# First stage of an RWKV + MoE kernel: the transposed FFN input is scaled from the transposed LayerNorm output, and the routing moves into its own round

## The reference

```python
xn = layernorm(x)                                  # no gain, eps 1e-5
prev = concat([xn[:, 1:2], xn[:, :-1]], axis=1)    # the token before
k, v, r, g = [(xn + (prev - xn) * tm_i) @ W_i.T for i in "kvrg"]
ek, ekv, gate = exp(k), exp(k) * v, sigmoid(r) * sigmoid(g)   # kept for the output stage
z = w_norm * xn * rsqrt(mean(xn**2) + 1e-6)        # input of the FFN, all 4096 tokens
probs = softmax(z @ w_router); top 4 of 32 experts  # each expert takes at most 256 tokens, in order
shared gate = sigmoid(z @ w_shared_gate)
```

## Time and profile before

| what | value |
|---|---|
| median of 3 runs | 1773.22 us (1773.07 to 1777.1) |
| the profiled execution, its own time | 1772.68 us |
| its span, first to last instruction | 1770.9 us |
| PE busy | 1690.1 us, 95% of the span |
| DVE, POOL, ACT busy | 1217.8, 878.3, 660.5 us |
| share of the chain that ended last | PE 79%, DVE 10%, waits for nothing shown 5% |

### The profile page before, as it was taken

The page is one execution under the profiler, slowest core; times in us unless marked ns, Lnnn a source line. Parts: engine busy times, 40 slices in busy tenths (PEclk is TensorE's granted clock), DMA queues, the critical chain, the costliest instruction groups (busy, mean ns, idle before and its releaser), DMA issues.

```text
span 1770.9 us, 26936 instructions
## 1 busy us (share of the span) xinstructions
PE 1690.1 (95%) x8752; PEld 1444.6 (82%) x8752; DVE 1217.8 (69%) x1798; ACT 660.5 (37%) x1086; POOL 878.3 (50%) x730
## 2 busy tenths in 40 slices
PE   4699999999889999999998899999999999999998
PEld 4578877788779999999997688888788888888887
DVE  4777778776635555555556978687686768778776
ACT  3344454454446566656653322112121212112121
POOL 2477887777635444544435635243252525344251
PEclk7799999999989999999999999999999999999999
DMA  6224434233366666666677656554554343343431
GB/s 225 95 72 159 152 131 154 103 136 119 127 228 245 248 229 222 245 248 229 222 260 238 208 186 208 169 170 155 172 167 164 125 140 122 122 157 108 149 109 46
DMA packets 130379, 299.36 MB, mean 169 GB/s; under 512 B 23724, under 2 KB 35116, under 8 KB 129776
## 3 DMA queue, kind: packets, MB, share of 16 engines
q1 hardware_dynamic: 110832, 264.58, 41.8%
q0 software_dynamic: 19456, 33.67, 6.7%
HBM read 233.57 MB, written 81.36 MB: 178 GB/s over the span
## 4 chain that ended last, share of the span: by engine, by line
PE 79%; DVE 10%; issue 5%; DMA 2%; POOL 1%; ACT 1%; DVEq 0%; SPq 0%; POOLq 0%; ACTq 0%
PE bank L1738 24%; PE bank L1116 15%; PE bank L1752 12%; PE bank L789 10%; PE bank L1143 8%; PE bank L1769 5%; PE bank L739 2%; PE bank L1108 2%; DVE mixf L553 2%; PE bank L757 1%; DVE st L518 1%; POOL slot_tokens L341 1%; DVE s_wg L1642 1%; DVE sr L572 1%; DVE s_ek L1586 0%
## 5 line engine op out<-in xcount | busy, mean ns | idle before, releaser
L789 PE MATMUL bank<-mix,w 128*128 128x512 f32 x1536 | 375.9, 402 | 25.9 <-POOL mix L333 12.8
L789 PEld LDWEIGHTS bank<-mix,w 128*128 128x128 f32 x1536 | 291.8, 193 | 93.2 <-issue 20.2
L1738 PE MATMUL bank<-s_zT,s_wg 128*128 128x512 f32 x1056 | 258.8, 395 | 9.8 <-DVE s_wg L1642 9.4
L1738 PE MATMUL bank<-s_zT,s_wu 128*128 128x512 f32 x1056 | 256.2, 392 | 2.8 <-DVE s_act_g L1547 1.9
L1752 PE MATMUL bank<-s_wd,s_h 128*128 128x512 f32 x1056 | 254.0, 389 | 0.8 <-DVE s_h L1553 0.8
L1738 PEld LDWEIGHTS bank<-s_zT,s_wg 128*128 128x128 f32 x1056 | 200.4, 190 | 54.6 <-DVE s_wg L1642 12.2
L1738 PEld LDWEIGHTS bank<-s_zT,s_wu 128*128 128x128 f32 x1056 | 199.4, 189 | 45.9 <-issue 2.3
L1752 PEld LDWEIGHTS bank<-s_wd,s_h 128*128 128x128 f32 x1056 | 198.3, 188 | 42.8 <-issue 1.2
L942 POOL TENSOR_TENSOR e_wg<-e_g_in,e_wg 128x1408 fp32r<-128x1408 f32 x32 | 103.5, 3233 | 219.4 <-ACT e_wg L967 219.4
L333 POOL TENSOR_TENSOR mix<-mixf,mix 128x512 fp32r<-128x512 f32 x120 | 156.6, 1334 | 68.6 <-ACT mix L413 68.1
L1373 POOL DMA_INDIRECT s_picked<-y_rows,s_slot x128 | 141.5, 1106 | 84.4 <-DVE s_total L1603 44.7
(11 more groups left out here) (149 smaller groups left out, 2388.4 us busy)
## 6 DMA issues: line engine op xcount, KB each, us to landing
s_wu<-wu_split SPq DMA_DIRECT2D x77, 512.0 KB, 3.4
e_g_in<-in_w_gate SPq DMA_DIRECT2D x32, 704.0 KB, 4.4
e_u_in<-in_w_up SPq DMA_DIRECT2D x32, 704.0 KB, 5.9
zT_tiles<-zT SPq DMA_DIRECT2D x32, 512.0 KB, 2.6
e_d_in<-in_w_down SPq DMA_DIRECT2D x32, 512.0 KB, 6.7
y_rows<-e_y SPq DMA_DIRECT2D x32, 512.0 KB, 2.9
s_zT<-zT_tiles SPq DMA_DIRECT2D x32, 512.0 KB, 5.9
x_in<-in_x SPq DMA_DIRECT2D x32, 256.0 KB, 4.2
```

Source lines behind the costliest of these rows:

```text
L789: last = pe.matmul(pj[m][:], w[i][:, w_part, k, m * P:(m + 1) * P], mix[:, i % 2, k, x_part, :], start=(k == 0 and q == 0), stop=(k == KC ...
L1738: last = pe.matmul(into[:], w[:, w_part, k, :], zT[:, :, x_part, k, :], start=(q == 0 and k == 0), stop=(q == 2 and k == KC - 1))
```

## The change

1. z is no longer transposed. xn is (now four tiles in SBUF, two PSUM banks in turn); r2 is turned once a round with four transposes of a broadcast column (`turn_r2`), and `make_zf` on DVE multiplies xnT, the norm weight as a per-partition scalar and the turned r2. High and low parts of all 512 tokens follow; they are stored as two parts of 1 MB.
2. The scores hold the router weights still (68 columns) and move 512 tokens: 8 matmuls a round. ACT copies the result to SBUF (`keep_score`), PE turns it back with four transposes (`turn_score`).
3. Scores, `choose`, `count` and `assign` of sequence b all run in round b. Scatters: 7 between the `mix_lo` calls of G and of the next K, 4 behind those, 5 in the next round. The last round has all 16 of its own, after 5 of round 6.
4. x is loaded two rounds ahead; r2 and the scales have two halves.
5. All small constants come in one array of 516 columns, loaded from ACT's queue; weights are loaded ahead of x of sequence 1. POOL makes the low parts of the R and G weights, behind `mix_lo` of V.
6. Expert 1's weights are loaded when R of the last round is done; the low part of expert 0's gate weight moves from POOL to DVE.

The core of the diff:

```diff
-        def z_lo(b, j):   # from tz, the transposed z in PSUM, by tile
+        def make_zf(b, half, k):
...
+            wait(dve, zl_made, n - 1)
+            dve.scalar_tensor_tensor(zf[:, k % 2, :], xnT[half][:, k, 1:T + 1], norm_col[:, k:k + 1], rb[:],
+                                     ALU.mult, ALU.mult).then_inc(zf_made, 1)
+        def make_zT(b, half):
+            make_zf(b, half, 0)
+            make_zf(b, half, 1)
+            z_lo(b, 0)
+            make_zf(b, half, 2)
+            z_lo(b, 1)
+            make_zf(b, half, 3)
+            z_lo(b, 2)
+            z_lo(b, 3)
...
# tensor
+        def turn_r2(b, half):
+            pe.wait_ge(pow_step, (b + 1) * POWS)
+            wait(pe, zf_made, b * KC)
+            for j in range(NT):
+                last = pe.transpose(rb[:, j * P:(j + 1) * P], r2[:, half, j:j + 1].to_broadcast([P, P]), ident)
+        def score(b):
+            pe.wait_ge(zl_made, (b + 1) * KC)
             for x_part in (1, 0):
                 for k in range(KC):
-                    last = pe.matmul(rp_lg[:, j * 2 * RW:(j + 1) * 2 * RW], zT[:, j % 2, x_part, k, :],
-                                     wr[:, k].rearrange("p q e -> p (q e)"),
+                    last = pe.matmul(sb, wr[:, k].rearrange("p q e -> p (q e)"), zT[x_part][:, k, :],
...
+        def one_round(b, half):
             project(b, K_, 0)
+            score(b)
             project(b, K_, 1)
+            turn_score(b)
             project(b, V_, 0)
+            turn_xn(b + 1, 0)
+            turn_xn(b + 1, 1)
             project(b, V_, 1)
+            count(b)
+            turn_xn(b + 1, 2)
+            turn_xn(b + 1, 3)
+            turn_r2(b + 1, 1 - half)
             project(b, R_, 0)
             project(b, R_, 1)
             project(b, G_, 0)
             project(b, G_, 1)
...
# gpsimd
+        def one_round(b, half):
+            mix_lo(b, V_)
+            norm_scales(b + 1, 1 - half)
+            mix_lo(b, R_)
+            scatter(b - 1, MORE, NT * TOPK)
+            mix_lo(b, G_)
+            scatter(b, 0, SOME)
+            mix_lo(b + 1, K_)
+            scatter(b, SOME, MORE)
+        def last_round():
+            mix_lo(LAST, V_)
+            scatter(LAST - 1, MORE, NT * TOPK)
+            mix_lo(LAST, R_)
+            scatter(LAST, 0, NT * TOPK)
+        SOME, MORE = 7, 11
...
# vector, one_round
+            make_gate(b - 1, 2)
+            make_gate(b - 1, 3)
             for k in range(KC):
                 make_mix(b, half, V_, k)
+            norm_stats(b + 1)
+            for k in range(KC):
+                make_mix(b, half, R_, k)
+            choose(b)
+            make_z(b + 1, 1 - half, 0)
+            make_z(b + 1, 1 - half, 1)
             make_ekv(b, 0)
             make_ekv(b, 1)
+            make_z(b + 1, 1 - half, 2)
+            make_z(b + 1, 1 - half, 3)
+            keep_scales(b + 1, 1 - half)
+            make_mix(b, half, G_, 0)
+            make_mix(b, half, G_, 1)
             make_ekv(b, 2)
             make_ekv(b, 3)
             make_mix(b, half, G_, 2)
             make_mix(b, half, G_, 3)
+            assign(b)
+            for k in range(KC):
+                shift_difference(b + 1, 1 - half, k)
+            for k in range(KC):
+                make_mix(b + 1, 1 - half, K_, k)
+            make_zT(b + 1, 1 - half)
             make_gate(b, 0)
             make_gate(b, 1)
...
# vector, last_round: V mixes, R mixes, choose, assign, ekv 0 and 1, G mixes, ekv 2 and 3, mix_lo of G, first_weights
...
# sync, expert stage
+        def second_weights():
+            sp.wait_ge(shared["r_done"], B * KC)
+            load(1, 1)
...
-            sp.wait_ge(gathered[0], 32)
-            sp.wait_ge(shared["g_done"], B * KC)
-            load(1, 1)
```

More of the change, by code:

```diff
@@ L350, in gpsimd @@
         pool.wait_ge(setup_pool, 4)
[L351 to L378, removed]
@@ L474, in one_round @@
                 mix_hi(b, R_, k)
[L475 to L487 removed]
+            make_xn(b + 1, 1 - half, 2)
@@ L661, in vector, with first_round @@
+        weight_lo(K_)
+        for j in range(3):
+            keep_turned(0, 0, j)
         for k in range(KC):
             shift_difference(0, 0, k)
[L663 removed]
             make_mix(0, 0, K_, k)
[L665 to L673 removed]
+        def first_round():
+            for k in range(KC):
+                make_mix(0, 0, V_, k)
+            weight_lo(V_)
+            make_zT(0, 0)
+            norm_stats(1)
+            keep_scales(0, 0)
+            dve.wait_ge(n_loaded, 16)
+            make_z(0, 0, 0)
+            make_z(0, 0, 1)
+            make_ekv(0, 0)
+            make_ekv(0, 1)
+            for k in range(KC):
+                make_mix(0, 0, R_, k)
+            make_z(0, 0, 2)
+            make_z(0, 0, 3)
+            make_ekv(0, 2)
+            make_ekv(0, 3)
+            choose(0)
+            for k in range(KC):
+                make_mix(0, 0, G_, k)
+            assign(0)
+            for k in range(KC):
+                shift_difference(1, 1, k)
+            make_mix(1, 1, K_, 0)
+            make_mix(1, 1, K_, 1)
+            make_gate(0, 0)
+            make_gate(0, 1)
+            make_mix(1, 1, K_, 2)
+            make_mix(1, 1, K_, 3)
+            make_zT(1, 1)
+            keep_scales(1, 1)
+            for j in range(NT):
+                make_z(1, 1, j)
@@ L687, in one_round @@
-            if not more:
-                for k in range(KC):
-                    mix_lo(b, R_, k)
+            norm_stats(b + 1)
+            for k in range(KC):
+                make_mix(b, half, R_, k)
+            choose(b)
+            make_z(b + 1, 1 - half, 0)
+            make_z(b + 1, 1 - half, 1)
             make_ekv(b, 0)
             make_ekv(b, 1)
-            if more:
-                z_lo(b + 1, 0)
-            if not before:
-                weight_lo(G_)
-                assign(b)
+            make_z(b + 1, 1 - half, 2)
@@ L708, in one_round @@
             make_mix(b, half, G_, 3)
-            if not more:
-                for k in range(KC):
-                    mix_lo(b, G_, k)
-                first_weights()
-            if more:
-                z_lo(b + 1, 2)
-                z_lo(b + 1, 3)
-                for k in range(KC):
-                    shift_difference(b + 1, 1 - half, k)
-                make_mix(b + 1, 1 - half, K_, 0)
-                make_mix(b + 1, 1 - half, K_, 1)
-                choose(b + 1)
+            assign(b)
```

646 lines of the change are left out of this document (372 added, 274 removed).

## The result

1764.13 us, median of 4 runs (1763.06 to 1766.36), against 1773.83 us (1773.07 to 1777.1) for the kernel before on the same chip: 0.9946 times, 95% interval 0.9931 to 0.9961. The change is faster, by 9.7 us where 56 were forecast, and the time lies outside the range of 1699 to 1740. The profiled execution took 1764.3 us, 1.8 outside its span.

A forecast was written before the change was run, and what follows sets the result against it. PE was taken to bound the rounds, with POOL and DVE not far below. 1772.7 - 37.7 (start) - 19.4 (middle rounds) + 8.2 (last round) - 7.4 (hand-over) = 1716.4, as a median 1717 us; range 1699 to 1740.

The forecast's parts named there:

- part 1: Middle rounds: 50.5 us each, between 48.8 and 54.1; six rounds 305 us against 324.4, a gain of 19.4 us.
- the 47.7 us of the DVE chain: Middle round: DVE's work from K0's start to the gate for the next K0, ending 1.1 us before PE needs it.
- I had added 3.5: Middle round, DVE up to the G mixes: 3.5 us for waits on POOL's SBUF turn and the store of z.
- rival 1: Middle rounds: DVE is the bound, `z_lo` and G mixes wait for whole POOL fours; 53 us a round, 1732; chance 0.18.
- Rival 2: Middle rounds: a new wait, K0's gate behind `make_zT`, eats the gain; period 54.1 us, 1738; chance 0.07.
- the 2 us of the prediction: Late in round 1: 2 us for a first score that finds zT late, DVE coming from a long round 0.
- Part 2: Start and round 0: K0 of round 0 at 20 us, of round 1 at 77 instead of 114.7; gain 37.7 us.
- Part 3: Last round: the slot table comes later, K0 to the end of the first turn takes 60 us; loss 8.2 us.
- Part 4: Hand-over to the experts: idle before expert 0's first down projection goes and it gets shorter; gain 7.4 us.
- rival 3: Round 0 stays long: K0 of round 1 at 88 us, 1728 in all; chance 0.10.
- rival 4: Slower than before: a 5.26 us gap with each scatter batch makes POOL's cycle 64.3 us, 1800; chance 0.04.

The follow-up runs named there:

- s9: The changed kernel with nine scatters instead of seven on POOL ahead of the four `mix_lo` of the next K; 1741.36 us.
- s9_ends: s9 with the last round's R low parts on DVE and, in round 0, four scatters ahead of round 1's K low parts; 1738.75 us.
- gates_s4_ends: Changed kernel with gates ahead of `make_zT`, four scatters before K's run, last R low parts on DVE, four round 0 scatters ahead of next K's `mix_lo`; 1757.56 us.
- g_weight_later: The changed kernel with POOL's low part of the G weight moved behind the low parts of R's input in round 0; 1763.45 us.
- late_w1: The changed kernel with expert 1's weights loaded after the gather of expert 0 and the end of G, as before the change; 1771.79 us.

## Why the prediction was wrong

**The step that failed** is in part 1, the order on DVE: "The last two `z_lo` of DVE lie in it. If they get in between two calls it costs 1.5 us, if they wait for all of them 4 us". With the 47.7 us of the DVE chain these are rounds of 49.2 and 51.7 us, and the 50.5 I took lies between them. Both were too short. In the round from K0 at 207.38 the stall is 5.1 us beyond the `z_lo`'s own length, a `z_lo` waits 0.45 us for its high part, and `make_zT` begins at 43.6 instead of 41.4: 47.7 + 2.2 + 0.4 + 5.1 = 55.4 us, the measured round. By my own times (`make_zT` from 41.4 on, POOL's run from 43.8 to 48.9) the second `z_lo` already lay in the run, and it is the one that is hit. The 2.2 us were lost although I had added 3.5: the turned scores come 1.6 us late, since K0 is slow, and runs of `mix_lo` hold `choose` (8.5 us for 5.3) and two mixes of G (2.85 us for 1.4). POOL's run begins at 47.0, 3.2 us late, for it waits for the slots; its seven scatters took the forecast time (9.2 us, 245.26 to 254.43, for 9.1). PE's work was right: from K0 to the end of G1 it is 50.3 us, of which the slow K0 makes 1.6 (7.2 us to the first score, 5.6 in s9), so 48.7 for my 48.8. That a late gate can also slow the clock was not priced.

The argument against rival 1 drew a wrong conclusion from a right reading. "Small DVE instructions of `assign` got in between POOL's calls" is what the kernel before shows, beside the run of four calls at 341.69:

```profile
341.86 1.15 DVE L621 SCALAR_TENSOR_TENSOR s<-idxf,bad 128x16 f32<-128x16 f32 x1
342.93 0.16 DVE L622 SCALAR_TENSOR_TENSOR s<-pos,second 128x16 f32<-128x16 f32 x1
343.24 1.04 DVE L624 CAST token<-keep_const 128x4 uint32<-128x4 f32 x1
344.19 0.16 DVE L625 TENSOR_TENSOR slot<-s,s 128x16 uint32<-128x16 f32 x1
```

The slots were ready after two of the four calls, but two of these instructions had each waited for the end of one call: they got in, and not for nothing. And it says nothing of a `z_lo` on 128x512. The row that was nearer to it, the mix that ended just after both `mix_lo` at 351.15, said that such an instruction can wait for the whole run. By the Trainium skill's GPSIMD Engine Reference, section Key points, DVE instructions in a 2-port perf mode or with two SBUF inputs contend with POOL. The runs agree for those with two SBUF inputs. They add that the wait of a `z_lo` lasts to the end of the run, where the steps of `seen`, three of the four, wait for one call each (1.15 to 1.22 us in the changed kernel). The 128x4 instruction of s9, with one input, waited for all four calls in round 7 and for one (1.06 to 1.08 us) in the rounds before. What decides between one call and the run is not shown.

**Rival 1 was the mechanism**, with 0.18; its size was 53 us a round where 55.4 were measured, and nothing in it for round 1, which took 68.3 us. Rival 2's 54.1 us were nearer, and its late gate behind `make_zT` is where PE waits, though for rival 1's reason. In round 1, eleven scatters (88.43 to 103.6) stand ahead of V's low parts, and a mix of R (its four take 6.23 us for 2.73) and the steps of `seen` are held by the next runs:

```profile
104.99 6.23 DVE L664 SCALAR_TENSOR_TENSOR mixf<-xx,keep_const,xnT 128x512 f32<-128x512 f32 x4 [0.63 <-POOL mix L356]
...
116.60 3.85 DVE L716 TENSOR_TENSOR seen<-seen,chosen 128x32 bf16<-128x32 bf16 x4
```

Moving four scatters gave 0.4 us in s9_ends and 1.9 in gates_s4_ends, so they are not the main cause. Of round 1's extra 13 us 9.3 are idle time of PE (14.4 us against 5.2): 2.3 for the first score, which finds zT late, as the 2 us of the prediction had it, 2.3 for the gate ahead of K1, 1.6 for xn, 6.5 for the gate ahead of K0 of round 2, and 1.7 in short ones. The other 3.6 us are PE's longer busy time (53.89 for 50.25 us). What an edit of the gate or of xn would win back was not tried.

**Part 2** was right in kind and 7 us short. The start missed by 1.3 us. In round 0 the scores came at 48.32 instead of 43: two `z_lo` took 3.81 and 4.21 us beside POOL's low parts of the R and G weights, the same mechanism in a second place, as g_weight_later shows for one of them. Which of the edits (packed constants, order of loads) brought the early start was argued from the trace and not tried.

**Part 3** held: 61.3 us against 60 (bounds 56.3 and 61.6), and the gap behind the first of the last round's scatters is there again, 2.94 us. **Part 4** held: 8.8 us by the marks, 7.7 by late_w1. Round 1 at 84 us lies between the forecast's 77 and rival 3's 88; rival 4 did not occur: scatters follow at 1.3 us.

The sum of the measured parts: -30.7 + 20.9 + 9.5 - 8.8 = -9.1 us, and the span fell by 8.4.

## What to carry to other kernels

Where GpSimd and VectorE both work in SBUF, draw the GpSimd runs as blocks on the time line. Of every VectorE instruction that would fall into a block, ask where its inputs are: with one in PSUM it kept its own length here; with two in SBUF it could take until the end of the call that it met (`seen`) or until the block's end (every `z_lo` of the middle rounds that met one), so price both. Then ask which of them stands ahead of what TensorE waits for. Moving the block by two independent instructions is a one-number edit and was worth 23 us of 1764 here, more than twice what the whole change brought; breaking it up was worth 13. If an engine has only a few us of room in a cycle, a busy time from an uncontended row is a lower bound, and the forecast should start at the rival.

## What the runs showed of the hardware

- A `z_lo` of 0.69 us took 5.82 us beside four POOL calls (5.00 us), 2.14 us beside one (1.32 us), 3.81 and 4.21 us beside one of 2048 columns (4.62 and 4.96 us). POOL's calls kept their 1.3 us there; where DVE's mixes came in between them they were longer too (3.44 us for two, at 265.97 in the changed kernel).
- The size does not free an instruction: one on 128x4 took 4.88 us. An input in PSUM does: the gate took 0.64 us each inside a run, and up to 490 us, in the traces of all 13 kernels with the change, none of 320 DVE instructions with an input in PSUM that began during a POOL call on low parts was longer for it, while all 50 `z_lo` that did were. The reductions with one input in SBUF kept their length as well (`chosen<-oh`, 1.13 us beside the run at 225.58). Indirect transfers started by POOL held no `z_lo` (0.69 us beside them).
- After 5.17 us of idle time on PE, 24 matmuls took 7.51 us instead of 5.75 in s9, so this wait was paid for 1.3 times. The length of the wait alone does not decide: behind almost the same wait K0 took 5.75 us in s9 (granted clock 1.00) and 7.33 us in s9_ends (0.76):

```profile
249.60 5.75 PE L928 MATMUL bank<-mix,w 128*128 128x512 f32 x24 [2.12 <-POOL mix L356]
```

```profile
249.33 7.33 PE L930 MATMUL bank<-mix,w 128*128 128x512 f32 x24 [2.13 <-POOL mix L356]
```
